# Another order within a quarter, last layers five quarters sooner, and ScalarE multiplies the embeddings by their factors

## What is computed

```python
e = stack([tbl_f[ids[:, f]] for f in range(26)], axis=1)              # 2048 x 26 x 64
x = layer_norm(dense @ Wd.T, gd, bd)                                  # 2048 x 128
y = layer_norm(einsum('bnd,ed->bne', e, Ws), gs, bs)                  # 2048 x 26 x 128
y = layer_norm(einsum('bne,pn->bep', y, Wsi), gsi, bsi)               # 2048 x 128 x 32
T = concatenate([x[:, None, :], swapaxes(y, 1, 2)], axis=1)           # 33 vectors of 128
Z = einsum('bnd,bmd->bnm', T, T)[:, TRIL_I, TRIL_J]                   # 528 products of pairs
z = layer_norm(Z @ Wl.T, gl, bl) * (arange(512) < 384)
h = relu(concatenate([z, dense], 1) @ W_top1 + b_top1)                # 512
h = relu(h @ W_top2 + b_top2)                                         # 256
out = h @ W_top3
```

## Time and profile before

| | |
|---|---|
| median of 3 runs | 1021.42 us (1021.18 to 1025.5) |
| profiled execution | 1019.76 us, its span 1018.0 us |
| PE (TensorE) busy | 657.4 us, 65% |
| PEld (weight loads) busy | 474.9 us, 47% |
| DVE (VectorE) busy | 530.4 us, 52% |
| ACT (ScalarE) busy | 279.4 us, 27% |
| POOL (GpSimd) busy | 423.3 us, 42% |
| mean granted TensorE clock | 0.79 |

### The profile page before, as it was taken

One profiled execution on the slowest core, in us unless ns is written; L12 is line 12 of the kernel. 1 busy time (PEld: TensorE's weight loads), 2 busy tenths in 40 slices (PEclk: granted clock), 3 DMA queues, 4 the chain that ended last, 5 costly groups with the idle time before them and its releaser, 6 DMA issues.

```text
span 1018.0 us, 17199 instructions
## 1 busy us (share of the span) xinstructions
PE 657.4 (65%) x6955; PEld 474.9 (47%) x6955; DVE 530.4 (52%) x769; ACT 279.4 (27%) x666; POOL 423.3 (42%) x422
## 2 busy tenths in 40 slices
PE   2034535364767757677775767768577776788887
PEld 2033324243444534446453545545355454566566
DVE  2248455454654535465453546545355654588740
ACT  1201122122232322233231323322132332345332
POOL 6757534545443344543345453433545343300000
PEclk9999676686776768777676778767687776799899
DMA  6111001010000011100001110000110010000000
GB/s 163 32 19 27 19 15 20 19 21 17 15 20 14 18 19 21 19 13 18 14 19 19 22 18 13 19 14 19 19 22 16 13 21 14 14 3 2 1 2 1
DMA packets 22606, 20.19 MB, mean 20 GB/s; under 512 B 12016, under 2 KB 14720, under 8 KB 22528
## 3 DMA queue, kind: packets, MB, share of 16 engines
q0 software_dynamic: 13312, 13.66, 7.4%
q1 hardware_dynamic: 8400, 4.33, 1.7%
q10 hardware_dynamic: 816, 1.11, 0.3%
HBM read 19.07 MB, written 0.01 MB: 19 GB/s over the span
## 4 chain that ended last, share of the span: by engine, by line
another core or an unknown queue 29%; PE 27%; issue 22%; DVE 14%; ACT 7%; ACTq 0%; DVEq 0%; POOL 0%; POOLq 0%
PE b_y L340 6%; PE b_l L416 5%; PE b_a L319 4%; DVE yb L781 3%; PE b_l L394 3%; DVE byn L776 2%; PE b_z L352 2%; ACT sq L508 2%; PE b_l L423 2%; DVE nrm L767 2%; PE b_mix L328 2%; DVE prod L747 1%; PE b_a L310 1%; ACT embt L492 1%
## 5 line engine op out<-in xcount | busy, mean ns | idle before, releaser
L253 POOL DMA_INDIRECT emb<-in_tbl,idx x416 | 422.6, 1016 | 453.7 <-DVE nrm L767 333.5
L319 PE MATMUL b_a<-gram_w,embt 128*128 128x128 f32 x416 | 85.3, 361 | 135.6 <-ACT embt L492 65.1
L793 DVE RECIPROCAL rstd_y<-std_y 128x32 f32<-128x32 f32 x64 | 21.2, 331 | 270.0 <-ACT std_y L513 269.9
L352 PE MATMUL b_z<-V 128*32 128x34 f32 x4096 | 91.3, 206 | 96.7 <-issue 89.6
L319 PEld LDWEIGHTS b_a<-gram_w,embt 128*128 128x128 f32 x416 | 71.9, 257 | 149.6 <-ACT embt L492 76.4
L508 ACT ACTIVATE sq<-yb 128x1024 f32<-128x1024 f32 x64 | 67.7, 1057 | 265.8 <-DVE yb L781 219.7
L328 PE MATMUL b_mix<-mix,byn 128*128 128x128 f32 x512 | 103.3, 334 | 39.8 <-issue 38.9
L352 PEld LDWEIGHTS b_z<-V 128*32 128x32 f32 x4096 | 67.6, 114 | 121.7 <-issue 107.8
L788 DVE TENSOR_REDUCE var_y<-sq 128x32 f32<-128x1024 f32 x64 | 78.1, 1220 | 71.9 <-ACT sq L508 47.2
L328 PEld LDWEIGHTS b_mix<-mix,byn 128*128 128x128 f32 x512 | 88.5, 239 | 48.3 <-issue 47.4
L340 PE MATMUL b_y<-mixed,projw 64*128 64x512 f32 x256 | 99.2, 862 | 15.2 <-ACT mixed L503 14.9
(11 more groups left out here) (131 smaller groups left out, 759.2 us busy)
## 6 DMA issues: line engine op xcount, KB each, us to landing
emb<-in_tbl,idx POOLq DMA_INDIRECT x416
dense<-in_r_dense_t SPq DMA_DIRECT2D x16, 128.0 KB
V<-in_L_rec_Wl ACTq DMA_DIRECT2D x1, 1056.0 KB
w<-in_W_top SPq DMA_DIRECT2D x2, 512.0 KB
w<-in_W_top SPq DMA_DIRECT2D x1, 768.0 KB
out_y<-y_sb SPq DMA_DIRECT2D x16, 0.5 KB
idx<-in_ids SPq DMA_DIRECT2D x1, 195.0 KB
wd<-in_L_rec_Wd SPq DMA_DIRECT2D x1, 128.0 KB
```

Of the source, the lines that this page charges most:

```text
L253: pool.indirect_dma_start(out=emb[t % 2][:, f, :], out_offset=None, in_=tables[f], in_offset=bass.IndirectOffsetOnAxis(ap=idx[:, t, f:f + ...
L319: last = nc.tensor.matmul(b_a[:, n * P:(n + 1) * P], embt[:, n, :], gram_w[:, :], start=True, stop=True)
L352: last = nc.tensor.matmul(b_z[32 * q:32 * q + 32, GRAM * j:GRAM * (j + 1)], v[:, 0:NP], v, start=True, stop=True)
```

## The change

The turns of the last steps move: by_sample and pair_rows, interact and moments_o one or two quarters sooner, layer1 to layer3 and the store five quarters sooner (78 quarters in place of 83). Within a quarter TensorE does mix_features ahead of transposes, and gram is moved from the end of the quarter to a place ahead of project; norms comes behind project and interact_back. On VectorE add_bias comes ahead of norms, scale is done in its own quarter and not in the next one, by_sample and shuffle are split in two. On ScalarE copy_mixed comes ahead of copy_embt, and deviation_y, copy_zs, scale_o, copy_z and scale_x are done sooner. normalize goes from VectorE to ScalarE: one activation for each feature with its factor as scale, at once after deviation_y of the second and of the fourth measured quarter; VectorE keeps the reciprocal (recip_n). `dt` has 4 buffers in place of 5, `xt` 2 in place of 3, and the waits that keep buffers apart are set accordingly. The diff, cut; deviation_x, deviation_y and deviation_o only change their place in the file.

```diff
-PAIRS = 12
-INTERACT = 13
-INTERACT_NORM = 14
-INTERACT_BACK = 15
-LAYER1 = 18
-LAYER2 = 20
-LAYER3 = 21
-STORE = 22
+PAIRS = 11
+INTERACT = 12
+INTERACT_NORM = 13
+LAYER1 = 13
+LAYER2 = 15
+LAYER3 = 16
+STORE = 17
...
             def dense_back(t):
                 pe.wait_ge(xn_done, t + 1)
+                after(pe, zt_copied, 2 * (t - 1))
                 nc.tensor.transpose(b_x[:, 3 * P:4 * P], xn[:, :], ident[:, :]).then_inc(xt_done, 1)
...
             def pair_rows(t):
 
                 pe.wait_ge(zb_ready, 3 * (t + 1))
-                after(pe, zz_copied, t)
+                after(pe, h1_relued, 4 * (t - 1) + 2)
...
-                pe.wait_ge(x_copied, 2 * min(t + 3, T))
+                pe.wait_ge(x_copied, 2 * (t + 1))
+                pe.wait_ge(xn_done, min(t + 3, T))
...
                     dst = b_l[k][:, (m % 2) * P:(m % 2 + 1) * P]
                     for n, c in enumerate((3, 4, 0, 1, 2)):
-                        rhs = dt[t % 5][:, c - 3, :] if c > 2 else z_t[:, c, :]
+                        rhs = dt[t % 4][:, c - 3, :] if c > 2 else z_t[:, c, :]
                         last = nc.tensor.matmul(dst, w1[:, c, m * P:(m + 1) * P], rhs, start=(n == 0), stop=(n == 4))
                 last.then_inc(h1_done, 1)
...
             def layer3(t):
                 pe.wait_ge(h2_relued, 2 * (t + 1))
-                pe.wait_ge(zt_copied, 2 * min(t + 3, T))
-                pe.wait_ge(zz_copied, min(t + 2, T))
+                pe.wait_ge(zt_copied, 2 * min(t + 2, T))
...
@@ -439,32 +432,32 @@
                     dense_back(t)
                 if (t := tile(h, DENSE)) is not None:
                     dense_transposes(t)
-                if ab:
-                    transposes(*ab)
                 if bc:
                     mix_features(*bc)
                 if ab:
-                    norms(*ab)
+                    transposes(*ab)
+                if cc:
+                    gram(*cc)
                 if bc:
                     project(*bc)
+                if (t := tile(h, INTERACT_NORM)) is not None:
+                    interact_back(t)
+                if ab:
+                    norms(*ab)
                 if (t := tile(h, LAYER2)) is not None:
                     layer2(t)
                 if (t := tile(h, PAIRS)) is not None:
                     pair_rows(t)
+                if (t := tile(h, LAYER3)) is not None:
+                    layer3(t)
                 if (t := tile(h, INTERACT)) is not None:
                     interact(t)
-                if (t := tile(h, LAYER3)) is not None:
-                    layer3(t)
                 if (t := tile(h, LAYER1)) is not None:
                     layer1(t, 0)
-                if (t := tile(h, INTERACT_BACK)) is not None:
-                    interact_back(t)
                 if (t := tile(h, LAYER1 + 1)) is not None:
                     layer1(t, 1)
                 if (t := tile(h, DENSE)) is not None:
                     dense_project(t)
-                if cc:
-                    gram(*cc)
...
+            def normalize(t, k):
+
+                act.wait_ge(rstdn_done, 2 * t + k + 1)
+                after(act, byn_ready, 2 * t)
+                for f in HALVES[k]:
+                    last = nc.scalar.activation(nrm[:, :, f], emb[t % 2][:, f, :], ACT.Copy, scale=rstd_n[:, f:f + 1])
+                last.then_inc(nrm_ready, 1)
...
-                ab, bc = part(h, MEASURE), part(h, PROJECT)
+                ab, bc, cc = part(h, MEASURE), part(h, PROJECT), part(h, PROJECT + 1)
                 if (t := tile(h, DENSE_BACK)) is not None:
                     copy_x(t)
+                if bc:
+                    copy_mixed(*bc)
                 if ab:
                     copy_embt(*ab)
-                if (last := part(h, PROJECT + 1)):
-                    deviation_y(*last)
+                if (t := tile(h, DENSE_NORM)) is not None:
+                    deviation_x(t)
                 if (t := tile(h, INTERACT_NORM)) is not None:
                     deviation_o(t)
+                if cc:
+                    copy_zs(*cc)
                 if (t := tile(h, DENSE_NORM)) is not None:
-                    deviation_x(t)
-                if bc:
-                    copy_mixed(*bc)
-                if (last := part(h, PROJECT + 2)):
-                    copy_zs(*last)
+                    scale_x(t)
+                if (t := tile(h, INTERACT_NORM)) is not None:
+                    scale_o(t)
                 if (t := tile(h, DENSE)) is not None:
                     copy_dt(t)
+                if (t := tile(h, INTERACT_NORM)) is not None:
+                    copy_z(t)
                 if bc:
                     square_y(*bc)
                 if ab and ab[1] % 2:
                     deviation_n(ab[0], ab[1] // 2)
+                if bc:
+                    deviation_y(*bc)
+                if ab and ab[1] % 2:
+                    normalize(ab[0], ab[1] // 2)
                 if (t := tile(h, LAYER2)) is not None:
                     relu2(t)
                 if (t := tile(h, PAIRS)) is not None:
@@ -615,14 +624,8 @@
                     copy_y(t)
                 if (t := tile(h, LAYER1)) is not None:
                     relu1(t, 0)
-                if (t := tile(h, INTERACT_NORM)) is not None:
-                    scale_o(t)
-                if (t := tile(h, INTERACT_BACK)) is not None:
-                    copy_z(t)
                 if (t := tile(h, LAYER1 + 1)) is not None:
                     relu1(t, 1)
-                if (t := tile(h, DENSE_NORM)) is not None:
-                    scale_x(t)
                 if h == 1:
...
-            def normalize(t, k):
-
+            def recip_n(t, k):
                 f0, n = HALVES[k][0], len(HALVES[k])
                 dve.wait_ge(stdn_done, 2 * t + k + 1)
                 after(dve, nrm_ready, 2 * (t - 1) + k + 1)
                 nc.vector.reciprocal(rstd_n[:, f0:f0 + n], std_n[:, f0:f0 + n]).then_inc(rstdn_done, 1)
-                dve.wait_ge(rstdn_done, 2 * t + k + 1)
-                after(dve, byn_ready, 2 * t)
-                nc.vector.tensor_tensor(nrm[:, :, f0:f0 + n].rearrange("p d n -> p n d"), emb[t % 2][:, f0:f0 + n, :],
-                                        rstd_n[:, f0:f0 + n].unsqueeze(2).broadcast_to([P, n, D]), ALU.mult).then_inc(nrm_ready, 1)
-
-            def shuffle(t):
-
+
+            def shuffle(t, k):
+
+                d = slice(k * D // 2, (k + 1) * D // 2)
...
-                for k in range(2):
-                    d = slice(k * D // 2, (k + 1) * D // 2)
-                    nc.vector.transpose(byn[t % 2][:, :, d].rearrange("p j d -> p d j"), nrm[:, d, :]).then_inc(byn_ready, 1)
+                nc.vector.transpose(byn[t % 2][:, :, d].rearrange("p j d -> p d j"), nrm[:, d, :]).then_inc(byn_ready, 1)
...
-            def by_sample(t):
-
-                dve.wait_ge(zs_copied, 4 * (t + 1))
-                after(dve, zt_done, 2 * t)
+            def by_sample(t, k):
...
+                if k == 0:
+                    dve.wait_ge(zs_copied, 4 * (t + 1))
+                    after(dve, zt_done, 2 * t)
...
+                else:
+
...
             for h in range(QUARTERS):
-                ab, bc, cc = part(h, MEASURE), part(h, PROJECT), part(h, PROJECT + 1)
-                if (t := tile(h, PAIRS)) is not None:
-                    by_sample(t)
+                ab, bc = part(h, MEASURE), part(h, PROJECT)
+
                 if (t := tile(h, INTERACT_NORM)) is not None:
                     moments_o(t)
                 if (t := tile(h, DENSE_NORM)) is not None:
                     moments_x(t)
-                    normalize(t, 0)
                 if (t := tile(h, SHUFFLE)) is not None:
-                    normalize(t, 1)
-                    shuffle(t)
-                if cc:
-                    scale(*cc)
+                    shuffle(t, 1)
+                if (t := tile(h, PAIRS)) is not None:
+                    by_sample(t, 0)
                 if (t := tile(h, INTERACT_NORM)) is not None:
                     recip_o(t)
                 if (t := tile(h, DENSE_NORM)) is not None:
                     recip_x(t)
+                if bc:
+                    add_bias(*bc)
+
                 if ab:
                     norms(*ab)
                     if ab[1] % 2:
                         bound_n(ab[0], ab[1] // 2)
                 if bc:
-                    add_bias(*bc)
                     variance(*bc)
+
+                if ab and ab[1] % 2:
+                    recip_n(ab[0], ab[1] // 2)
+                if (t := tile(h, PAIRS)) is not None:
+                    by_sample(t, 1)
+                if bc:
+                    scale(*bc)
+                if (t := tile(h, SHUFFLE - 1)) is not None:
+                    shuffle(t, 0)
```

More of the change, by code:

```diff
@@ L122, in tower @@
         dense = [sb(f"dense{h}", [P, DD]) for h in range(2)]
-        dt = [sb(f"dt{h}", [P, 2, P]) for h in range(5)]
+        dt = [sb(f"dt{h}", [P, 2, P]) for h in range(4)]
```

(33 more changed lines are left out.)

25 lines of the change are left out of this document (8 added, 17 removed).

## The result

The changed kernel takes 1086.39 us (median of 4 runs, 1084.48 to 1091.32) against 1021.3 us for the kernel before beside it: a ratio of 1.0641, 95% interval 1.0588 to 1.0693, 65 us longer. The prediction was 1055 us. The profiled execution has a span of 1082.7 us (before: 1018.0).

The account below looks back on a forecast made before the run. Waits, not VectorE's work, were taken to bound it: gathers that hold TensorE's marks late. A tile of 62.1 us against 59.5 gave +34 in 13 tiles, the ends +1: 1019.8 + 34 + 1 = 1055 us, range 960 to 1105.

Parts of the forecast that it names:

- Q0: First of a tile's four quarters, numbered by the batch measured in them; its gram was forecast to be caught by A.
- A: Gather of the 12 tables that wait for normalize(t, 1); forecast to start just before the gram of Q0.
- the 45% case: Main forecast, 45%: the gram of Q0 is caught by A; 1055 us, own range 1030 to 1085.
- The race: Gram against gather start: in Q0 the gram was to start at release+9, A at release+7.6, lost by 1.4 us.
- rival (1): 23%: the gram of Q0 gets through before A's data flows; 55.4 us a tile, 968 us.
- Gather B: Gather of the 14 tables waiting for normalize(t, 0); to catch the fourth quarter's gram 10 us after its start.
- B to release: Tile term: from the start of the 14-table gather until the held marks are seen, 21.0 us.
- release to A: Tile term: add_bias, product and sum, variance, root, 12 activations and POOL before A starts, 7.6 us.
- A to project's mark: Tile term: from A's start until project's mark is seen, between 13 and 17.7 us, taken as 14.5.
- the chain to V in Q0: Tile term: copy_zs, scale_o, interact_back, norms, product and sum, to the end of variance in Q0, 6.9 us.
- on to project of Q1: Tile term: root, reciprocal, scale, gram and project after the variance of Q0, 4.0 us with gaps.
- The ends: Seven quarters after the last gather +8 us, sooner last layers about 3+4 us less; together +1 us.

Follow-up runs that it names:

- Experiment 2: Changed kernel, with POOL's first gather of a tile also waiting for the first quarter's gram and its second for the third quarter's: 1026.91 us, ratio 1.0104.
- Experiment 1: Kernel before and changed kernel, both without the gathers of tiles 2 to 15, first chip: 714.0 us before, 774.8 after.
- experiment 9: Changed kernel as it is, on the third chip: 740.43 us against 669.73 for the kernel before, ratio 1.1060.
- experiment 4: Both kernels, each batch of tables (8, 6, 6, 6) gated behind its own quarter's gram, first chip: 820.35 us for the kernel before, 829.79 for the changed one.
- experiment 3: Changed kernel with the normalisation put back on VectorE behind its reciprocal, 26 ScalarE activations taken out, first chip: 1079.6 us, ratio 1.0622.
- experiment 7: Changed kernel without later gathers, second chip: norms put back ahead of interact_back, 737.8 us; then the gram put back behind project too, 746.6 us.
- experiment 6: Kernel before with four GpSimd waits for a gram, at tables 0, 7, 13 and 20, second chip: 670.03 us, ratio 0.9994.
- experiments 5: Kernel before with a gram written as 8 wide matmuls in place of 32, second chip: 671.04 us against 669.47 for the kernel before, ratio 1.0025.

## Why the prediction was right or wrong

- **The direction and the place were right.** The gram of Q0 was caught by A, as the 45% case said, and the grams of Q1 and Q2 were clear. The time, 1086, lies just above that case's own range (1030 to 1085) and the tile, 64.8, above its 61 to 63; 34 us were forecast for the steady tiles where 69 came.
- **The race** was closer than worked out: the gram started with the first table and not 1.4 us behind it. It was caught all the same. Experiment 2, which let it win, gave 1027 and not the 968 of rival (1).
- **Gather B** was mis-told. The gram of Q3 was to be caught 10 us after B's start; it came 18 us after it, behind the last table, held by dense_back's new wait for marks that were late without a gram. That the term, 21.0, came out as near as 22.6 is luck, and "a gram that is issued while a gather runs" is not the only thing behind which marks are late.
- **The terms**, predicted and measured in us: B to release 21.0, 22.6; release to A 7.6, 7.4; A to project's mark 14.5, 17.1; the chain to V in Q0 6.9, 6.2; on to project of Q1 4.0, 3.9; to V 3.9, 3.6; to B 4.2, 4.0. The sum is 64.8 where 62.1 stood, times 13 tiles 35 us: more than the 31 that the prediction was short of.
- **The mis-sized term** is A's start to project's mark. I went by tile 1, where a mark came before the gather's end; in the steady tiles it comes at the end, as the earlier trace rows had it. The 1.6 us in B's term lie in the late marks of layer2 and the pair rows (507.07, 511.34), after which Q3's gram could only start at 514.49.
- **The ends**: I had +1. The tiles give 13 times 5.3 = 69 us and the whole is 65, so the ends gave some 4 us back.
- **Where the attribution failed.** The step "what a change does to the time is read from two things: which gram falls into a gather, and how much work lies between" let the hold carry the answer. By the pieces of a tile, the two holds grew by 1.0 us (17.7 + 21.0 before, 17.1 + 22.6 after) and what lies between a release and the next gather by 4.2 (10.4 + 10.5, and 17.7 + 7.4). Experiment 1 loses 61 us without the later gathers, and experiment 9 loses 71 where no wait is "remote". So the new order has a length of its own, 5.2 to 5.8 us a tile. I had worked that term out (39 against 34.7 in the section on the ends, 40.9 measured) and used it for seven quarters only, as an end effect; times 13 it alone would have given +56 us.
- **The two do not simply add up.** With the gathers placed otherwise on the first chip, the new order costs 9 us (experiment 4) or stands within 9 us of the kernel before (experiment 2). So the 61 without gathers do not show that the 65 with them have the same cause: of the 65, the race with A, worth 59 in experiment 2, and the order's own length are two accounts of one loss, and no run parts them.
- **"The normalisation leaves VectorE: worth nothing by itself"** held on the first chip: experiment 3 moves it back for at most 7 us of 65.
- **Open**: which part of the order costs the 5.8 us. The wait of the norms behind z is next to none of it (experiment 7), and putting back other single parts made it worse. ScalarE's activations, with 12% of the chain the first candidate, were not put back without gathers or on the other kind of chip; nor were the sooner last layers. TensorE's granted clock is lower in the new order too (0.89 against 0.96 in experiment 1, and 0.88 against 0.95 in experiment 9); whether that is a cause or a result was not separated. The experiment on the gram's instructions did not meet the hold, so whether their number makes it was not settled.

## What to carry to other kernels

Take the longest-lasting disturbance out of both kernels before you argue how a change meets it: two runs without the gathers gave 61 us of difference where there were 65 with them. Then put it elsewhere in both as well: the gated pair differs by 9 us only, so a difference without the disturbance is not yet a share of the one with it. An order of instructions over five engines is one piece; a part of a good order, put into another, can cost more than it brings. Where one engine's marks come late beside a gather, start the gathers behind the burst of small instructions: one line took 19% off here, and the like of it, at other tables, cost nothing on a chip of the other kind.

## What the runs showed of the hardware

- **Chips differ by a third on the same kernel.** Before: 1016 to 1021 us on the first, 669 to 670 on the second and the third, single runs within 1% of their median. On the first, marks of TensorE come late while a gather runs (zs 12.8 us after the gram); on the third zs came 2.1 us after it, and no wait is "remote" in any of the six runs of the second and third. What makes the chips differ was not found out. The first chip loses in the first tile already: without later gathers, copy_embt of tile 1 comes 76.1 us behind that of tile 0 (experiment 1), on the second chip with them 31.0 (experiment 6).
- **On the first chip short gathers cost far less than long ones.** In the kernel before, the same 26 gathers a tile add 24 us in stretches of 12 and 14, and 9 us (44.4 less 35.2) in stretches of 6 to 8 that start behind a gram; in the changed kernel 24 and 3 (44.3 less 41.0).
- **On the second chip GpSimd's own time is near the bound of the old order**: in experiments 5 and 6 it waits for little but its own issue until the last table, and 26 gathers (1.36 us each with the 0.30 between them) are a tile. The tile without gathers is as long (35.2), so it is not the only bound.
